# Cross attention and state space unrolled, and maxima folded from 128 to 64 partitions before their transposes

## What is computed

```python
q, k = rmsnorm(q, q_norm_w), rmsnorm(k, k_norm_w)
scores = einsum('bhqd,bhkd->bhqk', q, k) * scale + mask
attn = softmax(scores, axis=-1)          # over the 1601 keys
out = einsum('bhqk,bhkd->bhqd', attn, v) @ o_proj_w.T
...
state = state * dA_t + dtx_t * B_t       # state space, per group and head
y_t = einsum('bhpn,bhn->bhp', state, C_t)
```

## Time and profile before

| | |
|---|---|
| median of 3 runs | 2383.8 us (2383.47 to 2384.16) |
| the profiled execution's own time | 2386.23 us |
| its span | 2384.5 us |
| PE busy | 97% of the span |
| DVE, POOL, ACT busy | 82%, 66%, 54% |
| mean granted TensorE clock | 0.989 of 2.4 GHz |

### The profile page before, as it was taken

How to read it: one execution, slowest core, us unless ns; L and a number is a source line. 1 busy time by engine, 2 the same in 40 slices (tenths; PEclk the granted TensorE clock), 3 DMA queues, 4 the chain that set the end, 5 groups by cost and what they waited for, 6 DMA issues and landing times. The chain is left out here.

```text
span 2384.5 us, 48515 instructions
## 1 busy us (share of the span) xinstructions
PE 2313.0 (97%) x18380; PEld 1666.4 (70%) x18380; DVE 1949.6 (82%) x2668; ACT 1277.4 (54%) x2066; POOL 1576.9 (66%) x1056
## 2 busy tenths in 40 slices
PE   7989999999999999999999999999999788999999
PEld 3557787778877787778877788778877344555555
DVE  6758888888888788888878888888879757888998
ACT  6845545554555445554545545554555436555654
POOL 0128888888888788888878888888878102443443
PEclk9989999999999999999999999999999999999999
DMA  6520000000100001000000100000001541211211
GB/s 215 183 63 26 28 26 26 26 28 18 34 26 25 27 26 34 18 28 26 26 27 27 32 26 26 26 28 10 10 26 63 180 166 45 80 62 62 79 47 44
DMA packets 101143, 117.71 MB, mean 49 GB/s; under 512 B 8238, under 2 KB 70830, under 8 KB 100910
## 3 DMA queue, kind: packets, MB, share of 16 engines
q1 hardware_dynamic: 98894, 107.25, 14.1%
q0 software_dynamic: 2016, 7.34, 1.1%
HBM read 96.74 MB, written 17.83 MB: 48 GB/s over the span
## 5 line engine op out<-in xcount | busy, mean ns | idle before, releaser
L177 POOL TENSOR_TENSOR p_l<-S,p_h 128x1792 f16<-128x1792 f32 x126 | 422.6, 3354 | 210.3 <-ACT p_h L472 210.3
L580 DVE SCALAR_TENSOR_TENSOR S<-pS,rk,mask 128x256 f32<-128x256 f32 x832 | 354.8, 477 | 139.4 <-PE pS L260 123.9
L260 PE MATMUL p_acc<-w_l,ctx_h 128*128 128x256 f16 (+1 forms) x1664 | 456.0, 274 | 0.0
L260 PE MATMUL p_acc<-w_h,ctx_h 128*128 128x256 f16 (+1 forms) x1664 | 455.9, 274 | 0.0
L260 PE MATMUL p_acc<-w_h,ctx_l 128*128 128x256 f16 (+1 forms) x1664 | 455.9, 274 | 0.0
L590 DVE TENSOR_REDUCE mx<-S 128x256 f32<-128x3328 f32 x64 | 382.5, 5976 | 2.2
L260 PE MATMUL p_acc<-ctx_h,w_h 128*128 128x400 f16 (+1 forms) x1024 | 341.4, 333 | 3.5 <-PEq L821 3.5
L260 PE MATMUL p_acc<-ctx_l,w_h 128*128 128x400 f16 (+1 forms) x1024 | 341.3, 333 | 0.0
L260 PE MATMUL p_acc<-ctx_h,w_l 128*128 128x400 f16 (+1 forms) x1024 | 340.6, 333 | 0.0
L454 ACT ACTIVATE v_h<-p_acc 128x512 f16<-128x512 f32 (+1 forms) x224 | 126.8, 566 | 387.2 <-PE p_acc L260 387.2
L682 POOL TENSOR_TENSOR sq_l<-sq_f,sq_h 128x400 f16<-128x400 f32 (+1 forms) x256 | 242.8, 948 | 70.3 <-ACT sq_h L446 70.3
(11 more groups left out here) (275 smaller groups left out, 5292.4 us busy)
## 6 DMA issues: line engine op xcount, KB each, us to landing
ctx_p<-ctxT_dram SPq DMA_DIRECT2D x42, 458.0 KB, 3.7
s_wst<-winG_dram SPq DMA_DIRECT2D x8, 1536.0 KB, 6.6
q_wst<-wqT_dram SPq DMA_DIRECT2D x8, 1024.0 KB, 7.0
o_scratch<-o_st SPq DMA_DIRECT2D x32, 256.0 KB, 2.4
s_wst<-winG_dram SPq DMA_DIRECT2D x8, 1024.0 KB, 5.3
m_wost<-woutG_dram SPq DMA_DIRECT2D x8, 1024.0 KB, 5.4
qh<-q_hi_scratch SPq DMA_DIRECT2D x64, 64.0 KB, 1.9
ql<-q_lo_scratch SPq DMA_DIRECT2D x64, 64.0 KB, 2.0
```

Source lines behind the costliest of these rows:

```text
L177: eng.tensor_tensor(p_l[:, s % 2, t0:t1, :], S[:, s % 2, t0:t1, :], p_h[:, s % 2, t0:t1, :], ALU.subtract).then_inc(pl_ok, 1)
L260: mm = pe.matmul(out, x, y, start=first and j == 0, stop=final and j == 2)
L580: ins = dve.scalar_tensor_tensor(out=S[:, s % 2, t, :].rearrange("p (r q) -> p r q", r=REP), in0=bank[:, t % 2, :].rearrange("p (r q) -> p ...
```

## The change

Three edits. `maximum` gets a second instruction: VectorE takes the maximum of `mx`'s upper 64 partitions into its lower 64, behind a wait for the reduce (new semaphore `mxa_ok`). `turn_maxima` then transposes 64 partitions, so each of its two matmuls streams 64 columns of `ident` in place of 128, and `overall` reduces 64 numbers per query in place of 128. And both loops, of cross attention and of the state space, are replaced by straight code for all batch rows and groups, so that no register is computed and no branch taken there.

```diff
@@ -113,6 +113,7 @@
         s_ok = sem("s_ok")
         s_out = sem("s_out")
         mx_ok = sem("mx_ok")
+        mxa_ok = sem("mxa_ok")
         idt = sem("idt")
         mt_ok = sem("mt_ok")
         top_ok = sem("top_ok")
@@ -148,11 +149,8 @@
 
         def loop(eng, body):
 
-            body(0, 0)
-            with eng.Fori(1, NB - 2, 2) as b:
-                body(b, 1)
-                body(b + 1, 0)
-            body(NB - 1, 1)
+            for b in range(NB):
+                body(b, b % 2)
 
         def before(b, s, n):
 
@@ -320,7 +318,7 @@
                 wait(pe, mx_ok, u + 1)
                 wait(pe, o_ok, 2 * (u - 1))
                 for h in range(2):
-                    mm = pe.transpose(pO[s % 2][:, 1, h * P:(h + 1) * P], mx[:, h * P:(h + 1) * P], ident[:, :])
+                    mm = pe.transpose(pO[s % 2][:, 1, h * 64:(h + 1) * 64], mx[0:64, h * P:(h + 1) * P], ident[0:64, 0:64])
                 mm.then_inc(mt_ok, 1)
 
             def spread_maxima(b, s):
@@ -587,11 +585,14 @@
             def maximum(b, s):
                 u = U * b + s
                 wait(dve, s_out, 7 * (u + 1))
-                dve.tensor_reduce(mx[:, :], S[:, s % 2, :, :].rearrange("p t q -> p q t"), AX.X, ALU.max).then_inc(mx_ok, 1)
+                dve.tensor_reduce(mx[:, :], S[:, s % 2, :, :].rearrange("p t q -> p q t"), AX.X, ALU.max).then_inc(mxa_ok, 1)
+
+                wait(dve, mxa_ok, u + 1)
+                dve.tensor_tensor(mx[0:64, :], mx[0:64, :], mx[64:P, :], ALU.max).then_inc(mx_ok, 1)
 
             def overall(b, s):
                 wait(dve, mt_ok, U * b + s + 1)
-                dve.tensor_reduce(top[:, :], pO[s % 2][:, 1, :].rearrange("p (h c) -> p h c", h=2), AX.X, ALU.max).then_inc(top_ok, 1)
+                dve.tensor_reduce(top[:, :], pO[s % 2][:, 1, 0:P].rearrange("p (h c) -> p h c", h=2), AX.X, ALU.max).then_inc(top_ok, 1)
 
             def subtract(b, s, h):
                 u = U * b + s
@@ -1392,13 +1393,8 @@
         block = ctx.enter_context(nc.Block())
 
         def loop(eng, body, last):
-
-            body(0, 0)
-            body(1, 1)
-            with eng.Fori(2, G - 3, 2) as g:
-                body(g, 0)
-                body(g + 1, 1)
-            body(G - 2, (G - 2) % 2)
+            for g in range(L):
+                body(g, g % 2)
             last(L, L % 2)
 
         def on(f, g, lag, *rest):
```

## The result

| | change | before |
|---|---|---|
| median | 2379.08 us (2378.01 to 2380.7, 13 runs) | 2384.16 us (2383.43 to 2387.96, 13 runs) |
| profiled execution, its span | 2380.68 us, 2378.7 us | 2386.23 us, 2384.5 us |

The ratio is 0.9976 (95% interval 0.9969 to 0.9984), a gain of 5.1 us.

The account below looks back on a forecast made before the run. TensorE was taken to bound cross attention with no gap. On the profile, 2386.2 - 7.7 + 0.4 + 0 - 3.8 = 2375.1; from the median, 2383.8 - 11.1 = 2372.7 us, range 2363.5 to 2379.0.

Parts of the forecast that it names:

- The branches in cross attention, -7.7: Cross attention loop: straight code removes two branches back, taking two batch rows from 217.10 to 213.20 us, -7.7 us.
- I take the upper end, since in the rows without a branch PEclk is 1.00: Cross attention: both stall and half clock behind each branch were counted as gained, upper end 7.8 us.
- the lower end of 4.0: Cross attention: only the two stalls gained, 2 x 2.0 us, if the clock were to dip anyway.
- it took 2.4 us more than the median of the runs: Whole kernel: the profiled execution of 2386.2 us against the median of 2383.8 us, from which the gain was subtracted.
- The fold, +0.4: VectorE's new maximum in the maxima: hidden in 62 of 64 units, +0.2 us each in the first and last.
- a dependent step of 128x256 follows its predecessor by 0.45 us: Price taken for VectorE's new maximum of 64 partitions: 0.45 us, or 0.35 if the pipeline hides a part.
- The transposes, 0: Maxima on TensorE: halved columns offset by changes to 64 rows at about 0.09 us, 0.01 us a unit, 0 in sum.
- The rival in which rows cost no change, 2363.7: Maxima: using 64 rows costs no mode change, gaining 0.15 us in each of 62 units, 9 us; chance 23%.
- The state space, -3.8: State space loop: straight code gains 1.34 us each in bodies 2 and 4, 0.58 each in 3 and 5.
- The 0.64 before `ramp`: State space body 4: TensorE waits 0.64 us for `ramp`, absent in body 6; straight code was to remove it.
- since body 6 is the same code as body 4: State space: body 6, already straight at 48.23 us, was the reason to take the full -3.8 us.
- The rival for this (17%): State space gains nothing, as waits depend on how GpSimd's and VectorE's steps meet: 2376.5 us; chance 17%.

Follow-up runs that it names:

- the 15 runs above: Timed runs of the unedited kernel before: 11 at 2382.4 to 2384.5 us, 4 at 2386.5 to 2387.95 us.
- the last experiment: spread_later with GpSimd's second-tile addition of the squares put ahead of its low part in the state space: 2367.89 us, ratio 0.9934.
- both_straight: The kernel before with both loops written out and the maxima as before: 2376.59 us, ratio 0.9966.
- spread_later: both_straight with the spread issued behind the first three matmuls of the next value job: 2370.93 us, ratio 0.9944.

## Why the prediction was wrong

- **The branches in cross attention, -7.7: the mechanism held, its size failed.** The step was "I take the upper end, since in the rows without a branch PEclk is 1.00". The measured part is 4.8 (interval 2.4 to 6.7), near the lower end of 4.0. The stall of 1.7 to 2.2 us is in all five profiles that have the loop; the 1.7 us at half clock behind it is in three of them. The two profiles without it put the two branches at 4.1 and 4.2 us over straight rows; the half clock in one execution of four or so would add some 0.9 to a mean (3.4 x 4/15, an estimate from the 15 runs above). The sum was made on a profile of the dearer kind, and its difference was taken from a median mostly of the other: "it took 2.4 us more than the median of the runs" said so, and was used as a constant to subtract.
- **The fold, +0.4: the step "a dependent step of 128x256 follows its predecessor by 0.45 us" failed.** It takes 1.52 us beside GpSimd. The row used for its price comes from the end, where GpSimd is idle. That 62 units hide it was right, by 0.16 us. The two bare units cost 1.3 us (row 0 0.39, the end 0.9) instead of 0.4. In the last the fold took 0.93 us and TensorE's wait for `mx` grew by 0.96, of which the shorter wait for `top` gave back 0.13. In the first the fold took the 0.42 forecast, but the wait grew by all of it (1.82 to 2.28), and next to nothing was given back (0.31 to 0.28). That GpSimd's addition holds the fold up is shown by its end, which lies 0.29 us behind GpSimd's in one unit and 0.28 in another with an addition of another length, and by the 0.42 alone; the other form of instruction is held alike. The Trainium skill (SBUF — State Buffer, "SBUF: two separate sides") says that VectorE with two SBUF inputs and GpSimd share a pair of ports, which one holds for its whole instruction: by that rule the trace agrees, 0.42 against 1.52 us.
- **The transposes, 0: right, mechanism and all.** The mode change for rows costs 0.10 us, as for columns; the unit is 0.01 us longer where the forecast had it 0.01 shorter, the batch row 0.08 (213.32 against 213.24). That the mode, and not the fold, eats the halved stream is shown by the kernel with full transposes, 0.05 us a unit faster. The rival in which rows cost no change, 2363.7, is out.
- **The state space, -3.8: half right.** Alone it measured -2.5; in its profile bodies 2 to 5 gained 1.6 us. The 0.64 before `ramp` was seen only with the loop (in five of six profiles that have it, in none of the eight without), so straight code takes it away; the 0.53 belongs to both. The step that failed is "since body 6 is the same code as body 4": that is so, but body 6 was short by chance. It takes 48.80 or 48.81 in three further profiles of before, and the last experiment shows that its length hung on the near tie. The reading of body 4 also left out that TensorE waits 0.39 for the squares there, so that the 0.64 alone was never the whole 1.34. The rival for this (17%) had named how GpSimd's and VectorE's steps meet, and that was right. That its time, 2376.5, lies within 2.6 us of the measurement is luck: it had the state space at 0 and the branches at 7.7.
- **The sum.** The three terms missed by 2.9 (branches), 2.0 (maxima, +2.4 for +0.4) and 1.3 us (state space), all to the same side, and nothing made up for them: 11.1 forecast, 5.1 measured.
- **What the parts leave open.** The maxima part costs 2.4 us, of which the two bare units (1.3) and the other six rows (6 x 0.08) explain 1.8. Where the state space begins, the profile of the change has a stretch at half clock of 6.8 us (columns as in the earlier trace rows), and that of before, at 2003.3, one of 3.4 us:

```profile
1997.90:2004.70 6.80, 6.30 (x29) 4.53 (x30) 4.88 (x12) 3.86 (x4) 0.00 (x0) 0.50 0.00 0
```

The state space up to the first equal point is 1.6 us longer there (90.95 against 89.31). With full transposes it is 87.62. These stretches differ between executions of one kernel, and one of 6.8 us stands there in three profiles without a fold too (one of before, `both_straight`, `spread_later`), so whether the fold moves them was not settled.

## What to carry to other kernels

Before a cost seen in one profile is subtracted from a median, compare the profile's own time with the spread of the runs: where it lies at one side, part of the cost is not in every execution, and the lower end is the better guess. A stretch that is short once, in code that is long elsewhere, needs the same care: here each of three further profiles of the kernel before has body 6 at 48.80 or 48.81. Price a new VectorE step with two inputs in SBUF from a row in which GpSimd runs as it will beside the new one, and count what is left of the slack as well as whether it suffices. A step that halves TensorE's columns by using half its rows pays a change of mode ahead (0.10 us here); here moving an independent job in front of the waiting matmul gained 5.7 us where the halving gained nothing.

## What the runs showed of the hardware

- A taken branch of this long loop stalls TensorE by 1.7 to 2.2 us each time (ten of ten in five profiles); a stretch of 3.4 us at 1.2 instead of 2.4 GHz behind it came in three of five profiles, with the same instructions ahead of it.
- VectorE's step with two SBUF inputs was held 1.1 us by GpSimd's addition (0.42 to 1.52 us), and in turn GpSimd's step was held 0.56 us by VectorE's (1.16 to 1.72). Which of the two is held in the state space goes by a hair: GpSimd's step ran free in all 19 pairs in which it started up to 0.034 us behind VectorE's, and was held in all 34 in which it started 0.035 us or more behind, and with that goes 0.56 us of TensorE's time in a body.
- Two float32 transposes of 64 rows and 64 columns, each way with a change of mode, take TensorE 0.05 us more than two of 128 rows and 128 columns (1.29 against 1.24 us).
